# A transformer stack on one core: norms of the last layer on VectorE, new instruction lists, and dummy matmuls in the tile size of the step behind them

## What is computed

```python
def _mha_layer(q, k, v, Wq, bq, Wk, bk, Wv, bv, gamma, beta):
    ...
    out = out + q
    return _layer_norm(out, gamma, beta)  # g * (x - mean) / (std + EPS) + b
enc = q
for i in range(3):
    enc = _mha_layer(q, k, v, Wq[i], bq[i], Wk[i], bk[i], Wv[i], bv[i], gamma[i], beta[i])
    enc = leaky_relu(enc @ Wff[i] + bff[i], negative_slope=0.2) + enc
    q, k, v = (enc, enc, enc)
return enc
```

## Time and profile before

| | |
|---|---|
| median of 3 runs | 1123.93 us (1123.82 to 1132.66) |
| the profiled execution | 1126.91 us, its span 1125.1 us |
| busy | PE 1041.3, weight loads 762.7, DVE 828.8, ACT 595.9, POOL 333.1 us |
| mean granted clock of PE | 0.983 |
| chain that ended last | PE 22%, DVE 22%, POOL 5%, ACT 2% in its parts that are named |

### The profile page before, as it was taken

How to read it: one execution, slowest core, us unless ns; L and a number is a source line. 1 busy time by engine, 2 the same in 40 slices (tenths; PEclk the granted TensorE clock), 3 DMA queues, 4 the chain that set the end, 5 groups by cost and what they waited for, 6 DMA issues and landing times.

```text
span 1125.1 us, 37457 instructions
## 1 busy us (share of the span) xinstructions
PE 1041.3 (93%) x16315; PEld 762.7 (68%) x16350; DVE 828.8 (74%) x2316; ACT 595.9 (53%) x857; POOL 333.1 (30%) x417
## 2 busy tenths in 40 slices
PE   7969889989999999989999999989999999999985
PEld 4648666657777776767676777656767777767664
DVE  5787889876476644788777878999576675669885
ACT  4425445555666455544554455545666655374552
POOL 4021145510110203354460312453100110235547
PEclk9989899989999999999999999999999999999999
DMA  7000000000000000000000000000000000000001
GB/s 248 3 20 22 2 3 3 2 1 3 2 3 2 2 12 10 20 2 2 1 20 2 22 3 3 2 2 2 2 2 3 2 2 3 1 1 2 1 1 39
DMA packets 13716, 13.54 MB, mean 12 GB/s; under 512 B 617, under 2 KB 13170, under 8 KB 13298
## 3 DMA queue, kind: packets, MB, share of 16 engines
q1 hardware_dynamic: 13554, 11.14, 3.1%
HBM read 9.04 MB, written 2.10 MB: 10 GB/s over the span
## 4 chain that ended last, share of the span: by engine, by line
PE 22%; DVE 22%; POOL 5%; issue 2%; ACT 2%; POOLq 0%; ACTq 0%; DVEq 0%
DVE mx L1285 5%; PE pair L687 5%; PE pair L915 3%; PE pair L886 3%; DVE stats L1032 3%; PE pair L881 3%; PE pair L756 2%; PE pair L674 2%; DVE Y L1088 1%; DVE Y L1042 1%; DVE Y L1050 1%; DVE X L1165 1%; DVE mv L1035 1%; PE pair L789 1%; DVE rq L1083 1%
## 5 line engine op out<-in xcount | busy, mean ns | idle before, releaser
L965 ACT ACTIVATE PT<-pair 128x1024 f32<-128x1024 f32 x184 | 183.4, 1026 | 149.8 <-PE pair L886 130.9
L1285 DVE TENSOR_REDUCE mx<-pair 128x16 f32<-128x1024 f32 x184 | 218.9, 1215 | 39.9 <-PE pair L886 39.5
L915 PEld LDWEIGHTS pair<-V,PT 128*64 128x64 f32 x5888 | 183.4, 138 | 33.6 <-issue 20.5
L915 PE MATMUL pair<-V,PT 128*64 128x32 f32 (+2 forms) x5888 | 197.4, 224 | 4.8 <-DVE Y L1088 2.0
L886 PEld LDWEIGHTS pair<-KQ 32*128 32x128 f32 (+3 forms) x4416 | 170.6, 158 | 40.4 <-issue 5.9
L886 PE MATMUL pair<-KQ 32*128 32x128 f32 (+3 forms) x4416 | 181.2, 255 | 3.0 <-DVE mx L1285 1.5
L687 PE MATMUL pair<-xf,W_all 128*128 128x512 f32 x336 | 176.9, 624 | 3.0 <-ACT xf L931 1.6
L1312 POOL TENSOR_SCALAR ve<-mv 128x4 f32<-128x4 f32 x64 | 16.3, 255 | 537.7 <-DVE mv L1035 506.8
L931 ACT ACTIVATE KQ<-pair,c 128x512 f32<-128x512 f32 x160 | 100.0, 688 | 66.2 <-PE pair L687 66.0
L663 PE MATMUL pair<-warm 128*128 128x512 bf16 x294 | 105.1, 391 | 9.2 <-ACT xf L931 1.6
L931 ACT ACTIVATE xf<-pair 128x512 f32<-128x512 f32 x80 | 47.5, 597 | 87.6 <-PE pair L674 87.3
(11 more groups left out here) (114 smaller groups left out, 1634.3 us busy)
## 6 DMA issues: line engine op xcount, KB each, us to landing
W_all<-weights SPq DMA_DIRECT2D x1, 2880.0 KB, 13.8
Xin<-x SPq DMA_DIRECT2D x8, 256.0 KB, 3.3
C<-ctx SPq DMA_DIRECT2D x8, 256.0 KB, 4.0
out<-X SPq DMA_DIRECT2D x8, 256.0 KB, 2.7
row<-rows SPq DMA_DIRECT2D x1, 1024.0 KB, 7.5
c<-const SPq DMA_DIRECT2D x1, 536.0 KB, 5.7
W_all<-weights SPq DMA_DIRECT2D x1, 192.0 KB, 2.9
c<-const SPq DMA_DIRECT2D x1, 80.5 KB, 1.9
```

The source lines that it names most:

```text
L915: mm = pe.matmul(outputs[s][r, at:at + n], p[:, u, b, side, :], V[:, first:first + n], start=True, stop=True)
L965: act.activation(PT[:, place, :], banks.of("B", a, s, v)[:], ACT.Exp, scale=float((D // (2 * PAIRS[a])) ** -0.5)).then_inc(*banks.drain((" ...
L1285: dve.tensor_reduce(dst, banks.of("A", a, s, v)[:].rearrange("p (u m t) -> p u m t", u=2, t=S), AX.X, ALU.max).then_inc(*banks.drain(("A", ...
```

## The change

- `fill` makes its matmuls in the tile size of the step behind it: four of 32x128 for `A` and `B` of layers 0 to 4 (it then takes both places of the step, not the first alone), two of 128x64 for `pv` and `v`, four of 128x32 for `maskrow` and `maxrow` of layers 5 to 7, and one of 128x128 for all others. Each matmul has 512 columns as before.
- In the last group's last step (layer 8), DVE does the norm's second pass (times the inverse deviation, plus beta) inside its own `n1`, behind a wait for POOL's deviation, and adds the leaky relu's result to X itself. POOL leaves these out; PE and SP wait for DVE's signals.
- ACT does one Copy of one element before its list, into a new tile `spare`.
- All four lists are new: the same steps in another order (POOL without the steps that went to DVE), other PSUM places, other fillings. The lists are cut here to their beginnings and ends and to the places spoken of.

```diff
@@ ORDER @@
 ORDER = {
     "PE": """
-        0.0.0 x@7+2; 0.0.1 x@6; 0.0.0 pq@7+1; 0.0.3 x@5+1; 0.0.0 pk@4+1; 0.0.1 pq@7+1; 0.0.0 pv@6; 0.0.2 x@4; 0.0.0
...
-        1.7.3 pv@7 maxrow@6; 1.7.2 v0@5 v1@4; 1.7.3 B0@0 v0@7+2 v1@6; 1.8.0 x1@5+1 ff@7+1; 1.8.1 x1@6+1; 1.8.2 x1@5
-        ff@7; 1.8.1 ff@6+1; 1.8.3 x1@5+2 ff@7+1
+        0.0.0 x@7; 0.0.1 x@6; 0.0.0 pq@7+1; 0.0.2 x@5; 0.0.0 pk@4+2; 0.0.3 x@5+1; 0.0.1 pq@7; 0.0.2 pq@6+1; 0.0.1 pk@4
...
+        pv@7+1; 1.7.2 v0@6 v1@5; 1.8.0 x1@4+1; 1.7.3 maxrow@7+1 B0@0+2 v0@5+1 v1@4+1; 1.8.1 x1@7+1; 1.8.0 ff@6+1;
+        1.8.2 x1@5+4; 1.8.1 ff@7; 1.8.2 ff@6+4; 1.8.3 x1@5 ff@7+3
...
     "DVE": """
...
-        lm lrow; 0.1.0 O0; 0.0.1 mrow; 0.0.3 lm; 0.0.2 mx0 mx1; 0.1.0 O1 split; 0.0.3 lrow; 0.0.2 mx2 mx3; 0.1.0 sum;
-        0.1.1 O0; 0.1.0 n1; 0.0.2 nm; 0.0.3 mx0; 0.0.2 mrow; 0.0.3 mx1; 0.1.0 qm nkv; 0.1.1 O1 sum; 0.0.3 mx2 mx3 nm;
...
-        1.7.1 mx0; 1.7.3 leaky; 1.7.1 nm mrow; 1.7.3 qm; 1.8.0 O0; 1.7.2 km; 1.8.0 O1; 1.7.2 lrow; 1.8.0 sum n1; 1.7.3
-        km; 1.8.1 O0 O1; 1.7.2 mx0 nm; 1.7.3 lrow; 1.7.2 mrow; 1.8.1 sum; 1.7.3 mx0 nm; 1.8.1 n1; 1.7.3 mrow; 1.8.2 O0
-        O1 sum n1; 1.8.3 O0 O1 sum; 1.8.0 leaky; 1.8.3 n1; 1.8.1 leaky; 1.8.2 leaky; 1.8.3 leaky
...
+        mx2 mx3; 0.0.2 lrow; 0.0.3 nz; 0.0.1 nm; 0.0.3 lm; 0.1.0 O0; 0.0.2 mx0 mx1; 0.1.0 O1; 0.0.3 lrow; 0.0.1 mrow;
+        0.1.0 split sum; 0.0.2 mx2 mx3; 0.1.1 O0; 0.0.2 nm; 0.1.0 n1; 0.1.1 O1; 0.0.2 mrow; 0.0.3 mx0; 0.1.0 qm nkv;
...
+        leaky; 1.7.1 mx0 nm; 1.7.2 qm; 1.8.0 O0; 1.7.3 leaky; 1.8.0 O1; 1.7.1 mrow; 1.8.0 sum; 1.7.3 qm; 1.7.2 km;
+        1.8.0 n1; 1.7.2 lrow; 1.7.3 km; 1.8.1 O0 O1; 1.7.2 mx0 nm; 1.7.3 lrow; 1.7.2 mrow; 1.8.1 sum; 1.7.3 mx0 nm;
+        1.8.1 n1; 1.8.2 O0 O1; 1.7.3 mrow; 1.8.2 sum n1; 1.8.3 O0 O1 sum; 1.8.0 leaky; 1.8.3 n1; 1.8.1 leaky; 1.8.2
+        leaky; 1.8.3 leaky
...
     "POOL": """
...
-        leaky; 1.7.1 sum n1; 1.7.0 leaky; 1.7.1 leaky; 1.7.2 sum n1; 1.7.3 sum n1; 1.7.2 leaky; 1.7.3 leaky; 1.8.0 sum
-        n1; 1.8.1 sum n1; 1.8.2 sum n1; 1.8.3 sum n1; 1.8.1 leaky; 1.8.0 leaky; 1.8.2 leaky; 1.8.3 leaky
...
+        1.6.2 leaky; 1.7.0 sum n1; 1.6.3 leaky; 1.7.1 sum; 1.7.0 leaky; 1.7.1 n1 leaky; 1.7.2 sum n1; 1.7.3 sum n1;
+        1.7.2 leaky; 1.7.3 leaky; 1.8.0 sum; 1.8.1 sum; 1.8.2 sum; 1.8.3 sum
...
@@ -552,6 +553,7 @@
         PT = sb("PT", [P, NPT, 1024])
         expo = sb("expo", [P, 3, NT])
         warm = sb("warm", [P, 128], BF16)
+        spare = sb("spare", [P, 1])
 
         section = Section(known)
         banks = Banks(ctx, nc, section)
@@ -644,7 +646,7 @@
                         sp.dma_start(C[s][:], c_g[section.group, s]).then_inc(*c_in[s].mark(by=16))
                 for section.group in range(GROUPS):
                     for s in range(STREAMS):
-                        sp.wait_ge(*pool.at("enc", 8, s))
+                        sp.wait_ge(*(vec if section.group == GROUPS - 1 else pool).at("enc", 8, s))
                         sp.dma_start(o_g[section.group, s], X[s][:]).then_inc(*x_out[s].mark(by=16))
                 for s in range(STREAMS):
                     sp.wait_ge(*x_out[s].at())
@@ -655,13 +657,19 @@
             def _(pe):
                 held, places = {}, []
 
-                def fill(n, width, *use):
+                def fill(n, width, rows_, columns_, *uses):
 
                     loaded(pool, "warm")
-                    held[use], = banks.take(pe, places[:1], width, use)
+                    held.update(zip(uses, banks.take(pe, places, width, *uses), strict=True))
                     for _ in range(n):
-                        pe.matmul(held[use][:, 0:FILL], warm[:], warm[:].unsqueeze(1).broadcast_to((P, FILL // 128, 128)),
-                                  start=True, stop=True)
+                        for k in range(P * P // (rows_ * columns_)):
+                            r = slice(32 * k, 32 * k + 32) if rows_ == 32 else slice(0, P)
+                            c = slice(columns_ * k, columns_ * k + columns_) if columns_ < P else slice(0, P)
+                            bank = held[uses[k // 2 if rows_ == 32 else 0]]
+                            at = 512 * (k % 2) if rows_ == 32 else 0
+                            pe.matmul(bank[c, at:at + FILL], warm[r, 0:columns_],
+                                      warm[r, :].unsqueeze(1).broadcast_to((rows_, FILL // 128, 128)),
+                                      start=True, stop=True)
 
                 def room(*use):
 
@@ -698,13 +706,14 @@
                     name, _, n = name.partition("+")
                     name, _, where = name.partition("@")
                     places[:] = map(int, where)
-                    if n:
-                        if name[0] in "AB":
-                            fill(int(n), 2, name[0], a, s, 2 * int(name[1]))
-                        elif name[0] == "v":
-                            fill(int(n), 1, "O", a, s, int(name[1]) // 2 if PAIRS[a] == 8 else int(name[1]))
-                        else:
-                            fill(int(n), 1, name, a, s)
+                    if n and name[0] in "AB":
+                        uses = [(name[0], a, s, 2 * int(name[1]) + k) for k in range(len(places))]
+                        fill(int(n), 2, 32 if PAIRS[a] == 8 else P, P, *uses)
+                    elif n and name[0] == "v":
+                        fill(int(n), 1, P, 64, ("O", a, s, int(name[1]) // 2 if PAIRS[a] == 8 else int(name[1])))
+                    elif n:
+                        tiny = name in ("maxrow", "maskrow") and PAIRS[a] == 2
+                        fill(int(n), 1, P, 32 if tiny else 64 if name == "pv" else P, (name, a, s))
                     use = (name, a, s)
                     if name in ("pq", "pk", "pv"):
                         loaded(w_in if a else w0_in)
@@ -725,7 +734,7 @@
                             pe.wait_ge(*pool.at("enc", a, s))
                         turn(X[s] if a else Xin[s], use)
                     elif name == "x1":
-                        pe.wait_ge(*pool.at("x1", a, s))
+                        pe.wait_ge(*(vec if a == 8 and section.group == GROUPS - 1 else pool).at("x1", a, s))
                         turn(X[s], use)
                     elif name == "q":
                         pe.wait_ge(*vec.at("q", a, s))
@@ -1022,6 +1031,9 @@
                         return spent.at(a, s, v, ago=ago)
                     return banks.ready("O", a, s, v // 2 if PAIRS[a] == 8 else 1, ago=ago)
 
+                section.group = 0
+                act.wait_ge(*pool.at("warm"))
+                act.activation(spare[:], warm[:, 0:1], ACT.Copy)
                 walk("ACT", step)
 
             @block.vector
@@ -1042,14 +1054,26 @@
                         dve.tensor_scalar(dst[:, j, :], src[:, j, :], mv[lane(tag)][:, j, 0:1], rstd[lane(tag)][:, j:j + 1],
                                           ALU.subtract, ALU.mult).then_inc(*vec.mark(*tag))
 
+                def final(a):
+
+                    return a == 8 and section.group == GROUPS - 1
+
                 def norm_affine(name, *tag):
 
-                    s = tag[-1]
+                    a, s = tag[1:]
+                    i = lane(tag)
                     dve.wait_ge(*vec.at("mv", *tag))
                     for j in range(NT):
-                        dve.scalar_tensor_tensor(out=Y[s][:, j, :], in0=X[s][:, j, :], scalar=mv[lane(tag)][:, j, 0:1],
+                        dve.scalar_tensor_tensor(out=Y[s][:, j, :], in0=X[s][:, j, :], scalar=mv[i][:, j, 0:1],
                                                  in1=rowb(name + "_g"), op0=ALU.subtract, op1=ALU.mult
                                                  ).then_inc(*vec.mark("scaled", *tag))
+                    if final(a):
+                        dve.wait_ge(*vec.at("scaled", *tag))
+                        dve.wait_ge(*pool.at("rstd", *tag))
+                        for j in range(NT):
+                            dve.scalar_tensor_tensor(out=X[s][:, j, :], in0=Y[s][:, j, :], scalar=rstd[i][:, j:j + 1],
+                                                     in1=rowb(name + "_b"), op0=ALU.mult, op1=ALU.add
+                                                     ).then_inc(*vec.mark(*tag))
 
                 def absent(sums, a, s):
 
@@ -1223,6 +1247,9 @@
                         y = Y[s].rearrange("p j c -> p (j c)")
                         dve.scalar_tensor_tensor(out=y, in0=banks.of(*use)[:, 0:TOK], scalar=1.0, in1=y, op0=ALU.mult,
                                                  op1=ALU.max).then_inc(*banks.drain(use, vec, "leaky", a, s))
+                        if final(a):
+                            dve.wait_ge(*vec.at("leaky", a, s))
+                            dve.tensor_tensor(X[s][:], X[s][:], Y[s][:], ALU.add).then_inc(*vec.mark("enc", a, s))
                     elif name[:4] == "silu":
 
                         c = int(name[4])
@@ -1349,7 +1376,8 @@
                     elif name == "kvstats":
                         deviation(False, "kv", a, s)
```

(8 more changed lines are left out.)

## The result

The changed kernel takes 1095.41 us (median of 4 runs, 1093.2 to 1097.97), the kernel before 1125.52 us (4 runs, 1123.82 to 1132.66). The ratio is 0.972, 95% interval 0.967 to 0.977: faster by 2.8%. Forecast were 1116 us and a range from 1102 to 1128. The direction is right, the size is not: -30 us, where the sum had -8.

A forecast was written before the change was run, and what follows sets the result against it. No engine is full: PE (93% busy) and DVE (74%) take turns setting the pace. Terms -5.5 - 3.3 + 0 - 1.1 + 1.9 = -8.0 us took the median of 1123.9 to 1116 us, range 1102 to 1128.

The forecast's parts named there:

- fillings in the tile of the next step: PE's list: 72 fewer changes of tile at 0.095 us, 81% of them counting: -5.5 us, bounds 0 and -6.8.
- 38 fewer fillings: PE's list: 256 fillings, 38 fewer at 0.216 us, 8.2 us in all, half given back: -3.3 us.
- `nm` ahead of `n1`: DVE's list, stream 2 ahead of next layer's 1.14 us `n1`, in PE's 3.96 us wait: -1.1 us, clock up to -5.
- all other moves in the lists: The remaining moves among PE's 648 and DVE's 540 moved steps: could not be priced, +-6 us kept for them.
- norms and adds on DVE: Last layer's tail: added second passes and waits for POOL's deviation against work given back: +1.9 us, bounds -2.9 and +4.
- early Copy: ACT's 1.28 us table load moves before the first data; it was hidden already: 0, bounds 0 and -1.3 us.
- The prediction's last sentence: Forecast is wrong first where new lists make unpriced waits: PE's idle time for DVE, not its fillings, will have moved.
- 81%: Share of PE's filling groups, 197 of 243, whose next step followed the last filling without more delay.
- the bound of -2.9: Tail norms on DVE: -2.9 us if waits of streams 0 to 2 fall where stream 3 isn't ready anyway.
- The gain stays off the path: Rival: PE waits where fillings or their changes of tile stood; 1121 to 1127, say 1124 us; chance 0.27.
- All of it lands: Rival: full gains of fillings, tiles, `nm`, clock, tail and Copy, -25 us: 1099, with half the extras 1105; chance 0.2.
- The rival on the clock: Rival: fewer fillings bare PE's idle gaps, the clock falls and the kernel slows, over 1127 us; chance 0.08.

The follow-up runs named there:

- nm_early: Kernel before, with only DVE's `nm` of stream 2 (layer 0, first group) moved ahead of the next layer's stream 0 `n1`: 1125.5 us, ratio 0.999.

## Why the prediction was wrong

| step | forecast us | shown, at equal clock |
|---|---|---|
| fillings in the tile of the next step | -5.5 | -3.4 (0 in the old lists) |
| 38 fewer fillings | -3.3 | -2.5 (38 x 0.065) |
| `nm` ahead of `n1` | -1.1 | -0.7 |
| all other moves in the lists | 0, +-6 | -20.6 (-23.8 + 2.5 + 0.7) |
| norms and adds on DVE | +1.9 | -2.1 (+5.0 in the old lists) |
| early Copy | 0 | 0 |

The sum of the right column is -29.3; the changed kernel stands 1121.2 - 1092.3 = 28.9 us below before at equal clock.

**The step that failed** is "the other moves I can't price; I keep +-6 for them". 648 of PE's 1072 steps and 540 of DVE's 849 had moved; that term was the change, and it was given the least room. What the runs showed in its place is -20.6 us, more than all other terms together, spread over both halves of the lists. The profile left room for it: PE was idle 83.8 us, one of its waits was 3.96 us, and the same trace has DVE's 5.67 and 5.52, which the prediction didn't look at. One such place, put in alone, gave 2.4 us of order in the trace and 1.6 in the runs. Which other places give the rest was not taken apart. The prediction's last sentence named the right spot, waits between the engines, but looked there for waits that the new lists make; they took waits away.

**Its parts.** The fillings were mis-sized by their share: 81% was read from whether the next step followed without delay, but a step that starts at once can still be early for a chain that waits further on (so I read it; no run shows it step by step). The counterpart without fillings shows a share of 0.065/0.216, about 30%, or some 40% if the slope out there is 0.5. Half of a filling for the 38 left out was nearer, by luck. The tile's side on the clock was taken for none; it took the 3.4 us back. The norms' step holds in the old lists, where stream 3's moments come 7.4 us later (forecast 4.9) and the end 1.9 sooner (forecast 2.95): I had worked it out on the old lists' gapless DVE and priced it for the new lists, where the bound of -2.9 was the truer case.

**The rivals.** "The gain stays off the path" was right for what it named, the fillings. "All of it lands" came out nearest in number, for another reason than its own. The rival on the clock didn't come: 28 us at the lower level in place of 31. What it said for the trace, that the gap of 3.96 us brings the clock down, nm_early doesn't bear out. The prediction's 24 us at the lower clock were those of three stretches; the whole span of before has 39, 2 x (1 - 0.9826) x 1125.1.

## What to carry to other kernels

Where several fixed lists are swapped at once, bound them by the idle time between the engines that a better order could reach, not by the one move that can be worked out; in this case the swap of the lists was the largest unknown and wanted the widest term. What an added instruction costs an engine depends on whether the list around it has gaps: at equal clock the same norms cost 5 us in one order and gave some 2 in another. And a dummy matmul is priced by the waits that it fills: its distance to the next start says what it occupies, and only leaving it out says what it costs.

## What the runs showed of the hardware

- A us of PE at 1.2 GHz cost this kernel 0.38 us over 61 executions, not the half that twice as long steps would suggest; single falls of 6.8 us cost 2.6 and 2.9, and of 3.4 us 1.3 to 1.6.
- The same kernel had 18 to 43 us at the lower clock in one execution and another, and this is most of its spread of 10 us.
- A matmul of 512 columns in another tile than the one before it cost 0.09 us more (0.306 to 0.309 from start to start against 0.215), for 32x128, 128x64 and 128x32 alike. Four of 128x32, two of 128x64 or four of 32x128 occupied no more than one of 128x128, 0.22 to 0.24 us.
- A dummy matmul that occupies 0.216 us was worth 0.05 to 0.07 us of time, estimated with the slope of 0.38. In the new lists tiled ones went with 15 to 37 us at the lower clock and whole ones with 7 to 20.
- Beside a POOL instruction small DVE operations were up to six times as long (`rq` 1.04 us, next to 1.04 us of POOL, against 0.17), an add of 128x512 twice (1.38 against 0.67).
